# First mixer: five of sixteen products on GpSimd with a DMA'd row of C, the divisor on a diagonal, rings of three and a later gate

## The reference, cut to what matters

```python
E, N, K, R = (256, 16, 4, 64)                     # channels, states, conv taps, rank of dt
A_log = log(arange(1, N + 1)) for every channel   # decay exp(dt * -exp(A_log))
x: (2, 2048, 256)
```

## Time and profile before

| | |
|---|---|
| runs of before | 4004.1, 4005.43, 3985.3 us; median 4004.1 us |
| profiled execution | 3994.4 us, of which the span is 3992.7 us (1.7 us lie around it) |
| granted PE clock, mean over the span | 0.887 |
| busy, whole span | PE 3117.2, DVE 2963.5, POOL 2159.3, ACT 1816.1 us |
| first mixer's units, sequence 0 | 148.1 to about 411 us of the span |
| the same, sequence 1 | 500.1 to about 763 us |

### The profile page before, as it was taken

One profiled execution on the slowest core, in us unless ns is written; L12 is line 12 of the kernel. 1 busy time (PEld: TensorE's weight loads), 2 busy tenths in 40 slices (PEclk: granted clock), 3 DMA queues, 4 the chain that ended last, 5 costly groups with the idle time before them and its releaser, 6 DMA issues. The chain is left out here.

```text
span 3992.7 us, 27893 instructions
## 1 busy us (share of the span) xinstructions
PE 3117.2 (78%) x7766; PEld 1390.4 (35%) x7766; DVE 2963.5 (74%) x2309; ACT 1816.1 (45%) x2415; POOL 2159.3 (54%) x902
## 2 busy tenths in 40 slices
PE   5666766678878587887988878879788787758999
PEld 2222222245566233332333333333233233234443
DVE  5889798722212599999999999999999999682121
ACT  4555455332202455554555555554545544362222
POOL 2555265300002288888788888888888888500000
PEclk7789789987757799998999989989999999989999
DMA  1000000123343244444445445444454545411110
GB/s 49 0 0 1 0 0 0 25 63 105 99 144 115 82 165 164 169 157 170 148 168 182 154 163 174 168 166 159 164 177 159 170 164 184 131 39 37 32 32 26
DMA packets 157712, 429.80 MB, mean 108 GB/s; under 512 B 22592, under 2 KB 51456, under 8 KB 157600
## 3 DMA queue, kind: packets, MB, share of 16 engines
q1 hardware_dynamic: 150688, 403.36, 30.4%
q0 software_dynamic: 6912, 25.17, 1.6%
HBM read 393.87 MB, written 34.60 MB: 107 GB/s over the span
## 5 line engine op out<-in xcount | busy, mean ns | idle before, releaser
L1204 POOL TENSOR_TENSOR mix_prod<-mix_spread,mix_h 128x1024 f32<-128x1024 f32 x512 | 1375.2, 2690 | 350.3 <-DVE mix_h L1628 229.7
L1723 PE MATMUL mix_banks<-mix_prod,kept_ident 128*128 128x512 f32 x2048 | 1101.0, 667 | 359.7 <-POOL mix_prod L1204 253.6
L1723 PEld LDWEIGHTS mix_banks<-mix_prod,kept_ident 128*128 128x128 f32 x2048 | 404.5, 208 | 942.4 <-POOL mix_prod L1204 411.4
L1253 ACT ACTIVATE mix_side_in<-mix_dt,mix_neg_a 128x1024 f32<-128x1024 f32 x384 | 438.2, 1141 | 338.8 <-DVE mix_h L1628 333.1
L1614 DVE TENSOR_TENSOR mix_banks<-mix_banks,mix_dtu 128x1024 f32<-128x1024 f32 x384 | 468.5, 1220 | 45.3 <-PE mix_banks L1713 41.7
L1628 DVE TENSOR_TENSOR_SCAN mix_h<-mix_side_in,mix_state,mix_banks 128x1024 f32<-128x1024 f32 x192 | 450.6, 2347 | 18.1 <-DVE mix_banks L1614 0.4
L1628 DVE TENSOR_TENSOR_SCAN mix_h<-mix_side_in,mix_banks 128x1024 f32<-128x1024 f32 x192 | 439.0, 2286 | 17.9 <-issue 0.9
L388 POOL TENSOR_TENSOR mix_drive<-mix_drive,mix_du 128x1024 f32<-128x1024 f32 x128 | 300.6, 2352 | 236.4 <-ACT mix_drive L441 236.4
L556 DVE TENSOR_TENSOR_SCAN mix_h<-mix_banks,mix_state,mix_drive 128x1024 f32<-128x1024 f32 x128 | 300.7, 2350 | 52.8 <-POOL mix_drive L388 35.9
L1213 POOL TENSOR_TENSOR mix_side_in<-mix_spread,mix_dtu 128x1024 f32<-128x1024 f32 x128 | 308.1, 2407 | 0.0
L1962 POOL DMA_DIRECT2D out<-finb_o x8 | 5.8, 728 | 521.3 <-DVE finb_eps L2101 521.3
(11 more groups left out here) (260 smaller groups left out, 4760.8 us busy)
## 6 DMA issues: line engine op xcount, KB each, us to landing
mix_spread<-c_rows SPq DMA_DIRECT2D x640, 512.0 KB, 3.8
exa_f<-f SPq DMA_DIRECT2D x32, 512.0 KB, 6.2
slot_outputs<-exa_inter POOLq DMA_DIRECT2D x32, 512.0 KB, 3.0
ln_zp<-slot_outputs SPq DMA_DIRECT2D x8, 2048.0 KB, 8.0
first_acc<-xT SPq DMA_DIRECT2D x8, 512.0 KB, 3.8
x_scratch<-first_acc POOLq DMA_DIRECT2D x8, 512.0 KB, 3.2
fw_scratch<-mix_res SPq DMA_DIRECT2D x8, 512.0 KB, 5.4
mix_lin<-fw_scratch SPq DMA_DIRECT2D x8, 512.0 KB, 5.2
```

What stands on the lines that cost most here:

```text
L1204: pool.tensor_tensor(prod[:, un % 2, :], spread[:, i % SLOTS, :], h[:, un % HR, :], ALU.mult).then_inc(prod_ready, 1)
L1253: act.activation(drive[un % 2] if pooled(un) else side_in[:, un % SR, :], dt[:, at // NS, :], ACT.Exp, scale=neg_a[:, way(p), at:at + 1]). ...
L1723: mm = pe.matmul(y_bank[:, hf, :], k.ident[:], half(prod[:, un % 2, :], hf), start=False, stop=True, skip_group_check=True)
```

## The change

Units whose state n is 2, 5, 8, 11 or 14 are "pooled": DVE makes no product for them. SP loads row n of C, spread over 128 partitions, into one buffer `c_row` (512 KB to SBUF) from a DRAM copy that it writes once per sequence; POOL multiplies `h` by it; ACT builds a 128 x 128 diagonal of `reff`; PE's `add` uses that diagonal as weights in place of the identity and makes no `chat` for such a unit. `drive` and `h` become rings of three, ACT writes the mask one unit ahead of the decay, and the state is saved only in the first half of the time (the second half does not need to save it). The gate moves behind product 0 of the next group. Two tiles are packed into one (`shared`) to make room.

```diff
-        self.drive = m.sb("drive", [P, 2, TC])
-        self.h = m.sb("h", [P, 2, TC])
+        self.drive = m.sb("drive", [P, 3, TC])
+        self.h = m.sb("h", [P, 3, TC])
...
+    BY_POOL = (2, 5, 8, 11, 14)
...
+            with sp.Fori(0, B) as b:
+                sp.wait_ge(par_kept, b * 2 + 2)
+                sp.dma_start(c0_rows[ds(b * NS, NS), :], rows[0:NS, :]).then_inc(rows_stored, 16)
+                sp.wait_ge(rows_stored, b * 16 + 16)
+                sp.sem_inc(rows_kept, 1)
+                for i in range(UNITS):
+                    if pooled(i):
+                        hf = blocks[i // NS][1]
+                        sp.wait_ge(pooled_ready, b * ALL_POOL + (1 + by_pool(i)))
+                        sp.dma_start(c_row[:], c0_rows[ds(b * NS + i % NS, 1), hf * TC:(hf + 1) * TC].broadcast_to((P, TC))
+                                     ).then_inc(row_loaded, 16)
...
+                def products(i):
+                    pool.wait_ge(r.scan_done, CREDIT + b * UNITS + (i + 1))
+                    pool.wait_ge(row_loaded, b * (16 * ALL_POOL) + 16 * (by_pool(i) + 1))
+                    pool.wait_ge(r.sum_done, CREDIT + b * UNITS + (i - 1))
+                    pool.tensor_tensor(r.prod[:, i % 2, :], r.h[:, i % 3, :], c_row[:], ALU.mult).then_inc(pooled_ready, 1)
+
+                drives(0)
+                for i in range(UNITS):
+                    if i + 1 < UNITS:
+                        drives(i + 1)
+                    if i and pooled(i - 1):
+                        products(i - 1)
...
+                def diagonal(i):
+                    at = blocks[i // NS][0] * NS + i % NS
+                    act.wait_ge(r.sum_done, CREDIT + b * UNITS + (i - 2))
+                    act.activation(diag[:, by_pool(i) % 2, :], k.ident[:], ACT.Copy,
+                                   scale=reff[:, at:at + 1]).then_inc(diag_ready, 1)
+
+                masked(0)
+                for i in range(UNITS):
+                    act.wait_ge(r.scan_done, CREDIT + b * UNITS + (i - 1) if i else CREDIT + b * UNITS)
+                    decays(i)
+                    if i + 1 < UNITS:
+                        masked(i + 1)
+                    if i:
+                        save_state(i - 1)
+                    if pooled(i):
+                        diagonal(i)
...
-                scans(0, 0)
-                for g in range(G):
-                    for n in range(1, NS):
-                        scans(g, n)
-                        if n == 1 and g:
-                            gate_y(g - 1)
-                        products(g, n - 1)
-                    if g + 1 < G:
-                        scans(g + 1, 0)
-                    products(g, NS - 1)
+                scans(0)
+                for i in range(UNITS):
+                    if i + 1 < UNITS:
+                        scans(i + 1)
+                    if not pooled(i):
+                        products(i)
+                    if i % NS == 0 and i:
+                        gate_y(i // NS - 1)
```

More of the change, by code:

```diff
@@ L306, in mixer0, with pooled, by_pool, by_dve @@
     H2 = L // TC
+    BY_POOL = (2, 5, 8, 11, 14)
+    def pooled(i):
+        return i % NS in BY_POOL
+    def by_pool(i):
+        return i // NS * len(BY_POOL) + sum(n < i % NS for n in BY_POOL)
+    def by_dve(i):
+        return i - by_pool(i)
+    ALL_POOL, ALL_DVE = by_pool(UNITS), by_dve(UNITS)
+    c0_rows = nc.dram_tensor("c0_rows", (B * NS, L), F32, kind="Internal").ap()
     blocks = [(c, hf) for c in range(C) for hf in range(H2)]
@@ L383, in _, with drives @@
                     pool.tensor_tensor(du[:, c, :], u[:, c, 1:L + 1], u[:, c, 0:L], ALU.subtract).then_inc(du_ready, 1)
-                for g in range(G):
[L385 to L389, removed]
+                def drives(i):
+                    pool.wait_ge(mask_ready, b * UNITS + (i + 1))
+                    pool.tensor_tensor(r.drive[:, i % 3, :], r.drive[:, i % 3, :], part(du, i // NS),
+                                       ALU.add).then_inc(r.drive_ready, 1)
+                def products(i):
[9 more added lines that the diff above has]
+                        products(i - 1)
         @block.scalar
@@ L434, in _ @@
                 act.wait_ge(step_ready, b + 1)
[L436 to L455, removed]
+                def masked(i):
+                    c = blocks[i // NS][0]
+                    at = c * NS + i % NS
+                    act.activation(r.drive[:, i % 3, :], part(dd, i // NS), ACT.Copy,
+                                   scale=mask[:, at:at + 1]).then_inc(mask_ready, 1)
@@ L559, in products, with scans @@
[L559 to L566, removed]
+                def scans(i):
+                    c, hf = blocks[i // NS]
+                    at = c * (NS + 1) + i % NS + 1
+                    dve.wait_ge(r.decay_ready, b * UNITS + (i + 1))
+                    dve.wait_ge(r.drive_ready, b * UNITS + (i + 1))
+                    if i >= 3:
+                        if pooled(i - 3):
+                            dve.wait_ge(pooled_ready, b * ALL_POOL + (1 + by_pool(i - 2)))
+                        else:
+                            dve.wait_ge(r.prod_ready, b * ALL_DVE + by_dve(i - 2))
+                        if not blocks[(i - 3) // NS][1]:
+                            dve.wait_ge(saved, b * (C * NS) + (blocks[(i - 3) // NS][0] * NS + (i - 3) % NS + 1))
+                    if hf:
+                        dve.wait_ge(saved, b * (C * NS) + (c * NS + i % NS + 1))
+                    dve.tensor_tensor_scan(r.h[:, i % 3, :], decay[i % 2], r.drive[:, i % 3, :], state[:, at:at + 1],
+                                           ALU.mult, ALU.add).then_inc(r.scan_done, 1)
@@ L663, in add @@
                     mm.then_inc(r.sum_done, 1)
[L665 to L674, removed]
-                        if n == 0 and g:
-                            pe.wait_ge(gated, b * G + g)
-                        add(g, n)
+                spread_c(0)
@@ new lines, in _ @@
+                for i in range(UNITS):
+                    if pooled(i):
+                        pe.wait_ge(pooled_ready, b * ALL_POOL + (1 + by_pool(i + 1)))
+                        pe.wait_ge(diag_ready, b * ALL_POOL + by_pool(i + 1))
+                    else:
+                        pe.wait_ge(r.prod_ready, b * ALL_DVE + by_dve(i + 1))
+                        after = i + 1 + pooled(i + 1)
+                        if after < UNITS:
+                            spread_c(after)
+                    if i % NS == 0 and i:
+                        pe.wait_ge(gated, b * G + i // NS)
+                    add(i)
```

67 lines of the change are left out of this document (40 added, 27 removed).

## The result

The change takes 3901.5 us in the median of four runs (3895.1 to 3903.9), the kernel before 4004.8 us in the same comparison. The ratio is 0.9746 with an interval of 0.9709 to 0.9783, so 2.5% faster. The forecast was 3925 us with a range of 3899 to 3962: right in sign and inside the range, but only 2.5 us above its lower end. The medians are 103 us apart and the profiled executions (3994.4 and 3901.4 us) 93 us, where 69.6 were forecast.

The account below looks back on a forecast made before the run. DVE was taken as the bound, busy 59.73 of 65.90 us in a group. Terms 54.4 + 16.6 + 9.8 - 7.2 - 4 = 69.6 us off the profiled 3994.4 gave 3925 us, range 3899 to 3962.

Parts of the forecast that it names:

- The best case of the sum: Whole kernel: nothing paid for gates and waits (3914 us), and 5 us more from last group's tail and small stalls: 3909.
- Rival 2: VectorE and GpSimd keep each other out, VectorE standing still while GpSimd multiplies: 23 us on, 4017 us; chance 0.02.
- Products leave: On DVE, 40 pooled units each cost 2.30 us in place of 3.66: 54.4 us off.
- More waits: On DVE, scans carry one or two more sequencer instructions: 4 us on.
- Border, scan: At six group borders, DVE's scan no longer idles 2.77 us for POOL's late drive: 16.6 us off.
- Border, gate: At group borders, the gate one product later no longer waits for PE's last add: 9.8 us off.
- The gate beside a busier POOL: At six borders, the gate's second instruction, reading two SBUF tiles, waits 1.2 us more beside POOL: 7.2 us on.
- Rival 1: POOL takes DVE's place as bound, with products at 3.3 us and handoffs not overlapping: 3947 us; chance 0.12.
- Rival 3: C's row comes late through one buffer; three units take round trip + 2.35 us: 4075 us at trip 11; chance 0.04.
- Rival 4: TensorE's clock falls behind pooled units, adds taking 3.6 us throughout: no gain, about 4000 us; chance 0.05.

Follow-up runs that it names:

- e9_before_h3: The kernel before with `h` as a ring of three, so scan i waits for product i-3 and not i-2: 3969.2 us, ratio 0.9917.
- e1_no_pooled: The change with no pooled unit, all 128 products on VectorE, no row loads or diagonals: 3957.6 us, ratio 0.9891.
- e12_diag_free: The change with ScalarE's diagonal waiting only for the add that last used its buffer, not the add three units back: 3909.4 us, ratio 0.9773.
- e5_row_after_row: The change with SP first loading the same row of C into an idle tile and waiting, before each row load: 3917.4 us, ratio 0.9808.
- e2_own_product: The change with scan i again waiting for product i-2 where VectorE made that one, rings of three kept: 3914.7 us, ratio 0.9781.

## Why the prediction was right, and where its sizes were off

*The number.* The direction and the bound were right; the size was short, and that the time fell inside the range is partly luck. The best case of the sum was 3909 us, and the profiled 3901.4 lies under it. It is inside only by the 10 us allowed for the spread of runs, and because 7.8 us of what the units lost came back outside them.

*The bound and the direction.* VectorE was the bound, and its products could leave without getting in each other's way: GpSimd's 40 products took 2352 ns in the median, scans and products kept 2.34 and 1.26. Rival 2, the warning of the Trainium skill's page Perfetto Trace Analysis, did not come true; the Trainium skill's page SBUF — State Buffer, section Who interferes with whom, says as much for one SBUF input, and these durations agree.

*"Products leave", 54.4 us.* Right as a sum of rows, wrong in its make-up. 1.36 us a product (3.66 - 2.30) held about 1.18 for the product itself (47.2 us for 40) and 0.21 of a wait on the own product; the step of 2.30, read at the start of a sequence, is 2.26 in the steady groups. The wait left all 128 units, not 40: measured 27.1 us (`e9_before_h3`) and 49.7 for the pooled products (`e1_no_pooled` to the change), 76.8 together. **This is the term that was mis-sized, by 22.4 us**: I read the 0.14 us between product and scan as the price of three waits, and had in the diff that scan i would wait for product i-3. 88 more steps of 0.21 are 18.5 of the 22.4. And the 49.7 hold 8.6 us that are not the products' but the gates', which met drives in `e1_no_pooled` and not in the change; put to the gates, they leave 68.2 here and make 32.4 of the next term.

*"More waits", 4 us on.* Nothing: the step is 1.18 us in `e9_before_h3`, without the added sequencer instructions, and in the change with them. The gap belonged to what was waited for, not to the number of waits.

*"Border, scan" and "Border, gate", 26.4 off, and "The gate beside a busier POOL", 7.2 on.* 19.2 forecast, 23.8 measured (`e9_before_h3` to `e1_no_pooled`). The idle times are gone as said, but the causes were given in part wrongly: not the mask ahead or the third buffer but, by elimination, the dropped wait on the saved state took the 2.77 us, and not the later gate but the drive in time took the 1.38. The price for the gate beside a busier GpSimd did not fall on VectorE: L638 took 1.23 us at all 8 places, and GpSimd's drive beside it 3.32 (207.86 in its timeline). That is luck of the order: in `e1_no_pooled`, `e5_row_after_row` and `e12_diag_free` it was VectorE that waited, 2.30 us in the mean.

The three differences are 22.4 + 4.6 + 4.0 = 31.0 us, and 69.6 + 31.0 = 100.6 is what the units lost.

*Rival 1* is half true: GpSimd is at 96% and sets 9.28 us cycles, but at 2.35 us a product, so late scans cost 7.3 us in all, of which 3.5 go with the diagonals' wait (`e12_diag_free`). *Rival 3* has its price right, but put the trip at 11 us, and it is 3.65. *Rival 4* did not come true, though with the drive in time the clock still falls at some borders: the adds there wait 1.79 us for the gate and then take 3.78, 1.98, 3.11, 3.78, 2.59 and 1.98 us at the six borders (the first at 209.04 in TensorE's timeline), the steady ones 1.88, and the granted clock of the two stretches above is 0.94 and 1.00. It costs little: beside the ends of the sequences VectorE waited 0.5 us for adds, GpSimd 7.7 us in 8 places.

## What to carry to other kernels

Ask of each wait how far back on the same engine the awaited instruction stands: one that is right ahead takes away the overlap of the two, and one more buffer gives it back. When work moves to a helper engine, give what feeds it a lead as well; the same lead that is worth nothing without the move (0.8 us) carried 94 us with it. And when both engines are full, the split is done: taking the fifth product of the sixteen back lost only 3 us, and a sixth on GpSimd lost 36, though how much of that is GpSimd and how much the diagonals' wait is open. A total that stands still can hide two effects, as in `e12_diag_free`: read the steps before calling an edit worth nothing.

## What the runs showed of the hardware that I had not expected

A VectorE scan that waits for the product just ahead of it starts 0.21 us later than one that waits for an earlier one (1.39 against 1.18 us after the product's start, the kernel before and `e9_before_h3`); in the change the same wait costs 0.19 us a step in the mean (`e2_own_product`). Without it the scan starts before the product's profiled end, 1.18 against 1.25 us. The Trainium skill's page Perfetto Trace Analysis, section Optimizing Scalar/DVE Operations, says that the write-acknowledgement half of an access overlaps with the next instruction; that fits, though no run here measures the acknowledgement itself. A VectorE instruction with two SBUF inputs took 1.23 us and GpSimd's drive beside it 3.32, or it took 3.38 us and the drive 2.35 (`e1_no_pooled`). In each case the one that started first kept its length: VectorE's at 207.75 against 207.86 in the change, GpSimd's at 212.38 against 212.43 in `e1_no_pooled`. ScalarE's 128 x 128 diagonal takes 0.40 us. A broadcast row of 512 KB makes its round trip through an idle queue in 3.65 us, 0.17 to the issue and 3.48 to the landing (`e5_row_after_row`).
